# Two heads per weight block in the attention scores, and later contexts written inside the first steps

## The reference, cut to what matters

```python
x, xn = X, layernorm(X)                     # X: 32 batches x 256 tokens x 128
ctx = xn @ We.T                             # 16 columns
scores = einsum('bhqd,bhkd->bhqk', Q, K) * 8**-0.5 + 0.1 * ctx @ ctx.T   # 16 heads of 8 columns
attn = softmax(scores)
x = x + (attn @ V) @ Wo.T + top-2-of-8 expert layer(xn)                   # 128 -> 512 -> 128
```

## Time and profile before

| | |
|---|---|
| three executions | 710.49, 710.17, 706.68 us, median 710.17 |
| profiled execution | 709.09 us, its span 707.3 us |
| granted TensorE clock, mean | 0.979 |
| attention, batches 0 to 15 | about 80 to 303 us |
| experts | about 303 to 492 us |
| attention, batches 16 to 31 | about 492 us to the end |

### The profile page before, as it was taken

The page is one execution under the profiler, slowest core; times in us unless marked ns, Lnnn a source line. Parts: engine busy times, 40 slices in busy tenths (PEclk is TensorE's granted clock), DMA queues, the critical chain, the costliest instruction groups (busy, mean ns, idle before and its releaser), DMA issues.

```text
span 707.3 us, 24553 instructions
## 1 busy us (share of the span) xinstructions
PE 648.5 (92%) x7800; PEld 433.7 (61%) x7800; DVE 614.3 (87%) x1106; ACT 541.5 (77%) x1123; POOL 467.4 (66%) x542
## 2 busy tenths in 40 slices
PE   0377899999999999989999999999999999999996
PEld 0264345555555555579999999998455555555553
DVE  8989789899999999868888888888999999999991
ACT  2592378888888888788888888888778877878775
POOL 8680468676687757135565565565687888778774
PEclk9986799999999999999999999999999999999999
DMA  8859556766766766684554454452667788787742
GB/s 244 318 161 331 151 146 167 203 180 171 194 171 183 202 172 175 155 132 93 107 107 94 106 101 106 100 107 70 148 165 186 179 185 183 175 185 186 178 112 79
DMA packets 162948, 113.32 MB, mean 160 GB/s; under 512 B 72625, under 2 KB 150449, under 8 KB 162865
## 3 DMA queue, kind: packets, MB, share of 16 engines
q1 hardware_dynamic: 153632, 90.63, 52.5%
q0 software_dynamic: 8192, 16.86, 9.7%
q10 hardware_dynamic: 1040, 4.76, 1.8%
HBM read 55.42 MB, written 47.19 MB: 145 GB/s over the span
## 4 chain that ended last, share of the span: by engine, by line
PE 70%; DVE 12%; SPq 6%; DMA 4%; issue 4%; ACT 3%; ACTq 0%; DVEq 0%
PE bank L1133 14%; PE bank L1251 14%; PE bank L1111 13%; PE mx L1240 13%; PE mx L1145 8%; DVE mx L955 5%; DMA stack<-qk_dram 3%; PE bank L1031 3%; PE bank L1193 2%; DVE A L790 2%; PE bank L1155 1%; PE bank L1162 1%; ACT A L707 1%; SPq L318 1%; DMA stack<-mT 1%
## 5 line engine op out<-in xcount | busy, mean ns | idle before, releaser
L707 ACT ACTIVATE A<-bank 128x512 f32<-128x512 f32 x502 | 278.3, 597 | 63.6 <-PE bank L1133 55.9
L955 DVE TENSOR_REDUCE mx<-mx 128x4 f16<-128x1024 f32 x256 | 302.6, 1205 | 20.0 <-PE mx L1145 14.5
L578 POOL TENSOR_SCALAR rows<-rows,slot_p 128x128 f32<-128x128 f32 x142 | 112.0, 798 | 95.8 <-DVE rows L1008 95.8
L1133 PE MATMUL bank<-stack 113*128 113x256 f16 x1004 | 170.7, 277 | 1.7 <-ACT A L707 0.8
L564 POOL DMA_INDIRECT slots_x<-rows,pos x128 | 123.6, 966 | 52.9 <-PE bank L1133 34.0
L608 POOL DMA_INDIRECT rows<-slots_y,pos x128 | 121.3, 948 | 40.8 <-PE bank L1133 19.7
L1111 PE MATMUL bank<-A,V 128*32 128x256 f32 x2048 | 137.3, 386 | 1.7 <-ACT A L707 1.6
L751 ACT ACTIVATE rows<-mx,b 128x256 f32<-128x256 f32 x284 | 111.5, 474 | 25.7 <-PE mx L1240 23.9
L1133 PEld LDWEIGHTS bank<-stack 113*128 113x128 f16 x1004 | 72.9, 98 | 89.4 <-ACT A L707 56.4
L1000 DVE TENSOR_TENSOR rows<-rows 128x512 f16<-128x512 f32 x142 | 101.1, 713 | 25.1 <-ACT rows L755 22.6
L1251 PE MATMUL bank<-w,rows 128*128 x1704 | 107.3, 219 | 1.3 <-DVE rows L1000 1.3
(11 more groups left out here) (142 smaller groups left out, 596.2 us busy)
## 6 DMA issues: line engine op xcount, KB each, us to landing
stack<-ctx_rest SPq DMA_DIRECT2D x64, 256.0 KB
stack<-qk_dram SPq DMA_DIRECT2D x128, 96.0 KB
slots_y<-rows SPq DMA_DIRECT2D x71, 128.0 KB, 2.0
qk_dram<-hi_qk SPq DMA_DIRECT2D x64, 128.0 KB
stack<-ctx_high SPq DMA_DIRECT2D x128, 64.0 KB
slots_x<-A ACTq DMA_DIRECT2D x1, 4644.0 KB, 19.8
w_stage<-in_w SPq DMA_DIRECT2D x8, 512.0 KB
qk_dram<-lo_qk SPq DMA_DIRECT2D x64, 64.0 KB
```

What stands on the lines that cost most here:

```text
L578: ins = pool.tensor_scalar(ye[n % 4][:, h, :], ye[n % 4][:, h, :], slot_p[:, n // 4 % 3, n % 4, h:h + 1], None, ALU.mult)
L707: act.activation(A[:, n % NA, :, :].rearrange("p h s -> p (h s)"), scores(k, n)[:, :], ACT.Exp, scale=SCALE).then_inc(s_xp, 1)
L955: dve.tensor_reduce(mx[:, a, 8 * qt:8 * qt + 8].rearrange("q (i e w) -> q i e w", i=2, e=2)[:, :, g % 2], MX[u % 2][:, :].rearrange("q (i ...
L1133: mm = pe.matmul(scores(k, n)[:, i * S:(i + 1) * S], stack[0:SHIFT + 1, par, h, 1, c * P:(c + 1) * P], stack[0:SHIFT + 1, par, h, 0, :], s ...
```

## The change

`stack` becomes, per side, six blocks of four heads: four query blocks (one for each half and class) and two key blocks, one for each half. A key block holds, for w = 0 to 3, the keys of head w (class 0) on its rows and of head w+4 (class 1) on its rows. One matmul takes 128 keys of both as weights and streams 512 columns, head w's queries and then head w+4's; the zeros of each query side drop the other head's keys. A score tile has 512 columns as before; tile p of a pair now holds heads w and w+4 where it held two neighbours of one class, and the values pick them accordingly. The plain products keep their four matmuls.

`load` makes six transfers: `ctx_rest` to the queries (128 KB in runs of 512 bytes) and to the keys (64 KB in runs of 512 bytes) instead of one of 256 KB in runs of 1024 bytes; high contexts and projections as before in bytes, in runs of 2048 bytes. `context` writes `ctx_high` four times over instead of twice (1024 KB in all, before 768 KB). `part_c` has a buffer of its own. `context(1)`, `(2)` and `(3)` are issued at the end of the steps k = -1, 0 and 1, and SyncE waits for all of them at the end of step 1. All clears are issued by ScalarE, in two transfers, at the start. The first scatter of rows by GpSimd waits for 18 score tiles instead of 10.

```diff
-START = 4
+START = 8
-        qk_dram = nc.dram_tensor("qk_dram", [2, 3 * DK, H * 2 * S], ...)
-        ctx_high = nc.dram_tensor("ctx_high", [2, B // 2, 2 * DE, 2 * S], ...)
+        qk_dram = nc.dram_tensor("qk_dram", [2, 2, 3 * DK, H * S], ...)
+        ctx_high = nc.dram_tensor("ctx_high", [2, B // 2, 2 * DE, 4 * S], ...)
-        stack = sb("stack", [P, 2, H, 2, S], F16)
+        stack = sb("stack", [P, 2, 6, 4, S], F16)
+        part_c = sb("part_c", [P, 4, 2, 2 * S], F16)
...
+        def both_sides(row, n, par, g, i):
+            first_, second_ = 2 * g + i, 4 + g
+            return stack[row:row + n, par, first_:second_ + 1:second_ - first_, :, :]
...
-                    sp.dma_start(high, hi.to_broadcast([P, 2, S])).then_inc(s_cw[r], 16)
+                    sp.dma_start(high, hi.to_broadcast([P, 4, S])).then_inc(s_cw[r], 16)
...
             def load(half2, par2, g):
-                sp.dma_start(stack[REST:REST + 2 * DE, par2, 8 * g:8 * g + 8, :, :], rest).then_inc(s_st[par2][g], 16)
+                sp.dma_start(dst, rest[:, :, 0:S].to_broadcast([2 * DE, 8, S])).then_inc(s_st[par2][g], 16)
+                sp.dma_start(stack[REST:REST + 2 * DE, par2, 4 + g, :, :], rest[:, :, S:2 * S].to_broadcast([2 * DE, 4, S])).then_inc(s_st[par2][g], 16)
...
             write(0, 1, 1)
-            clear(sp, 8, 10)
             context(0)
             sp.wait_ge(s_cw[0], 96)
             for g in range(2):
                 load(0, 0, g)
             write(1, 2, 2)
-            clear(sp, 10, 14)
-            context(1)
-            clear(sp, 14, 16)
-            context(2)
-            context(3)
...
-                if k == 1:
-                    for r in range(1, 4):
-                        sp.wait_ge(s_cw[r], 96)
                 for g in range(2):
...
                         write(par3, n_hq, n_lq)
+                if k in (-1, 0, 1):
+                    context(k + 2)
+                if k == 1:
+                    for r in range(1, 4):
+                        sp.wait_ge(s_cw[r], 96)
...
-                pool.memset(stack[64:P, par, :, 1, :], -1.0).then_inc(s_post, 1)
+                pool.memset(stack[64:P, par, 4:6, :, :], -1.0).then_inc(s_post, 1)
...
             clear(act, 0, 8)
             for g in range(3):
                 normalise(g)
+            clear(act, 8, 16)
             root(1)
...
-                classes = stack[:, par].rearrange("r (a i h) s t -> r i a h s t", a=2, i=2)
+                classes = stack[:, par, 0:4].rearrange("r (a i) h t -> r i a (h t)", i=2)
                 dve.memset(classes[0:64, 1], 0.0)
-                ins = dve.memset(classes[64:P, 0, :, :, 0], 0.0)
+                ins = dve.memset(classes[64:P, 0], 0.0)
...
-                        for i in range(2):
-                            h = 8 * (g // 2) + 4 * p + 2 * (g % 2) + i
-                            mm = pe.matmul(scores(k, n)[:, i * S:(i + 1) * S], stack[0:SHIFT + 1, par, h, 1, c * P:(c + 1) * P], stack[0:SHIFT + 1, par, h, 0, :], start=True, stop=True)
-                        mm.then_inc(s_ex, 1)
+                        h, w = 8 * (g // 2), 2 * (g % 2) + p
+                        pe.matmul(scores(k, n)[:, :], k_side(par, h + w)[0:SHIFT + 1, c * P:(c + 1) * P], stack[0:SHIFT + 1, par, h // 4:h // 4 + 2, w, :], start=True, stop=True).then_inc(s_ex, 1)
```

More of the change, by code:

```diff
@@ L240, in scores, with q_side, k_side @@
             return ring[n % len(ring)] if k == B - 1 else EX[n % 2]
+        def q_side(par, h):
+            return stack[:, par, h // 4, h % 4, :]
+        def k_side(par, h):
+            return stack[:, par, 4 + h // 8, h % 4, :]
+        def both_sides(row, n, par, g, i):
+            first_, second_ = 2 * g + i, 4 + g
+            return stack[row:row + n, par, first_:second_ + 1:second_ - first_, :, :]
         def head_values(par, c, g, i):
@@ L314, in context @@
                 for q in range(2):
-                    lo, hi = (part_c[r][:, a:a + 1, q * S:(q + 1) * S] for a in range(2))
+                    lo, hi = (part_c[:, r, a:a + 1, q * S:(q + 1) * S] for a in range(2))
                     high, rest = (c[q, 4 * r:4 * r + 4].rearrange("i c (m t) -> (i c) m t", t=S) for c in (ctx_high, ctx_rest))
-                    sp.dma_start(high, hi.to_broadcast([P, 2, S])).then_inc(s_cw[r], 16)
+                    sp.dma_start(high, hi.to_broadcast([P, 4, S])).then_inc(s_cw[r], 16)
                     sp.dma_start(rest[:, 1:3], hi.to_broadcast([P, 2, S])).then_inc(s_cw[r], 16)
@@ L403, in attend @@
                     if g == 0 and f["p"]:
-                        n_hq, n_lq, n_st = (v if isinstance(v, int) else sp.to_reg(v) for v in (b3_ + 1, b3_ + 1, 80 * half3))
+                        n_hq, n_lq, n_st = (v if isinstance(v, int) else sp.to_reg(v) for v in (b3_ + 1, b3_ + 1, 96 * half3))
                         if k is None or b3_ >= 2:
@@ L700, in attend @@
                             if k == 0 and n == 0:
-                                act.wait_ge(s_zero, 64)
+                                act.wait_ge(s_zero, 32)
                             if k != 0 or g >= 2:
                                 act.wait_ge(s_pv, 4 * b + g - 1)
-                            if k == 0 and n == NA // 2:
-                                for sm in s_cw:
-                                    act.wait_ge(sm, 96)
                             act.activation(A[:, n % NA, :, :].rearrange("p h s -> p (h s)"), scores(k, n)[:, :], ACT.Exp, scale=SCALE).then_inc(s_xp, 1)
@@ L1110, in values @@
                         for i in range(4):
-                            mm = pe.matmul(PV[32 * i:32 * i + 32, 0:S], head_values(pp, c, g, i), A[:, (4 * g + 2 * c + i // 2) % NA, i % 2, :],
+                            mm = pe.matmul(PV[32 * i:32 * i + 32, 0:S], head_values(pp, c, g, i), A[:, (4 * g + 2 * c + i % 2) % NA, i // 2, :],
                                            start=(e == 0 and c == 0), stop=(e == 1 and c == 1))
@@ L1144, in plain @@
                                 h = 8 * (v // 4) + 4 * i + 2 * (v // 2 % 2) + p
-                                mm = pe.matmul(MX[v % 2][:, (2 * i + p) * S:(2 * i + p + 1) * S], stack[r0:r1, par1, h, 0, v % 2 * P:(v % 2 + 1) * P], stack[r0:r1, par1, h, 1, :],
+                                mm = pe.matmul(MX[v % 2][:, (2 * i + p) * S:(2 * i + p + 1) * S], q_side(par1, h)[r0:r1, v % 2 * P:(v % 2 + 1) * P], k_side(par1, h)[r0:r1, :],
                                                start=True, stop=True)
```

35 lines of the change are left out of this document (17 added, 18 removed).

## The result

The changed kernel takes 719.18 us (median of 4 executions, 718.45 to 721.4), the kernel before, run on the same chip, 710.33 us: ratio 1.0138, 95% interval 1.0116 to 1.016. The forecast was 708.9 us, with a range from 703.5 to 715. The profiled execution took 718.94 us, its span is 717.2 us, so it is 9.9 us above the span before.

The account below looks back on a forecast made before the run. VectorE was taken to bound about 28 of 32 steps, SyncE's queue the start. From the profiled 709.09 us, -3.8 at the start and +2.5 for contexts gave 707.8, or 708.9 us for the median; range 703.5 to 715.

Parts of the forecast that it names:

- steady steps and product: Steady steps stay at 13.2 us, VectorE at 12.4; the 512-column product, its weight loads already hidden, gains 0.
- the rivals of TensorE's: Steady steps: VectorE's gap closes, 14 us gained (chance 0.05), or weight loads aren't hidden, the skill's rule, 28 us (0.03).
- The scatters' 0: GpSimd's scatters start 8 score tiles later and cost nothing, GpSimd having nearly 3 us free in a step.
- six transfers at 0: Loads: one more issue, 0.4 us, covered by VectorE's 0.6 us, costs 0; rival: 8.4 us lost (chance 0.12).
- What the contexts cost in their new place: Contexts 2 and 3 make loads 1.7 and 2.0 us late; 2.5 us lost after cover, bounds 0 and 7.7.
- The contexts block the queue: Rival, SyncE's queue: issues at 0.96 us, two steps 7.7 us late in all, 714.7 us (chance 0.12).
- over 5 us of SyncE for a context: Sign, SyncE's queue: the prediction is wrong if a context takes over 5 us of SyncE.
- the start, -3.8 us: Before the steady steps: memsets 1.7, VectorE's earlier start 1.1 and TensorE's clock 1.0 gain 3.8 us together.
- Memsets, 1.7: First microseconds: halved memsets of VectorE and GpSimd gain 0 to 3.0 us, taken as 1.7; X must have landed.
- The clear moved to ScalarE, 0: Start: the larger clear on ScalarE's queue costs 0, its bytes flowing before and while context 0 is written.
- ScalarE held up between 18 and 33 us: Sign, start: the prediction is wrong if the second clear holds up ScalarE between 18 and 33 us.
- TensorE's stand, 1.1, and its clock, 1.0: Start of batch 1: TensorE's 3.39 us stand goes, VectorE starts 1.1 us earlier; keeping the clock gains 1.0 us.

Follow-up runs that it names:

- e10: e6 with the 512-column product made as two matmuls of 256 columns again: 710.62 us, ratio 1.0029 to the kernel before.
- e1: Changed kernel with clears and contexts 1 to 3 back in their old places; new layout, six transfers and 512-column product kept: 711.8 us, ratio 1.001.
- e8: e4 with the 128 KB transfer of each load cut in two, a seventh transfer: 721.82 us, ratio 1.0163.
- e4: Changed kernel with contexts 1 to 3 issued behind the first load of step -1, their wait at the start of step 1: 709.93 us, ratio 0.9989.
- e12: e4 with contexts 2 and 3 written once more, to unread memory without a wait, at the ends of steps 0 and 1: 715.5 us, ratio 1.0084.
- e11: e4 with the second clear cut in two, batch 3's slots cleared by ScalarE in step -1 at 69.9 us: 708.24 us, ratio 0.9982.
- e6: Changed kernel with contexts 1 to 3 before the steps, as in the kernel before; clears stay as changed: 710.3 us, ratio 1.0002.
- e5: e4 with ScalarE's second clear issued later, at 49 us: 711.55 us, ratio 1.003.
- e2: Changed kernel with ScalarE's second clear issued later, behind batch 1's projections: 714.92 us, ratio 1.0066.
- e3: Changed kernel with the wait for the contexts' landing put before the later loads instead of the end of step 1: 719.11 us, ratio 1.0105.
- e7: e4, but context 3 and the wait for it stay at the end of step 1: 716.89 us, ratio 1.0085.
- e13: e11 with context 3 issued by ScalarE at 65.0 us instead of by SyncE: 707.89 us, ratio 0.999.

## Why the prediction was wrong

**Right: steady steps and product.** The step is unchanged (13.20 us, VectorE 12.41); e10 shows the product's 0 in isolation, and with it that the rivals of TensorE's had nothing in them. The scatters' 0 was never tested alone; e1 contains it. On the rule of the Trainium skill that was weighed, "TensorE: Matmul & The Clock Gate", section "The mechanism", e10 bears too: the same weights loaded again for the second 256 columns, on the same rows, cost nothing in a steady step, so here the measurement goes against it. Where VectorE sets the pace this alone couldn't show the load hidden, but two score tiles take 0.61 us with four loads and 0.60 with two.

**Right, but narrowly: six transfers at 0.** e1 gives 0.1% with an interval from -0.1 to 0.3, and the steady steps in the second half have no loss. But e8 shows how little was left: the cover was thin, as the text said, and the next 0.4 us cost 4.4 us by the profiles, 11.9 by the medians.

**Wrong: "What the contexts cost in their new place", 2.5 us.** It is 6.9 us in the profiles (e4 against after), 9.3 by the medians. The failed step is how the two contexts were added up; the landing was too short as well. SyncE's queue, with e4 as the same kernel without the contexts there:

| us | e4 | e12, copies | after |
|---|---|---|---|
| load behind context 2 | 102.84 | 104.59 | 104.97 |
| load of the second half | 108.98 | 111.06 | 111.49 |
| `shift_rows` of that half over | 113.02 | 116.43 | 117.16 |
| load behind context 3 | 116.71 | 121.52 | 123.69 |
| first plain product of batch 4 | 123.0 | 126.6 | 129.4 |

Context 2 made the load 2.1 us late; I had said 1.7, and of it 1.0 us is lost up to batch 3 (14.4 us from batch 2 to 3, in e4 13.4), where I had 1.1. But I let that lateness end there, and gave context 3 the full pause of 3.3 us. In fact the lateness stays on the queue: 2.1, 2.5, and with one issue of 1.99 us 4.1 us late at 117.16, so that the pause (3.7 us in e4) is used up before context 3 begins. The issues of a context took 4.0 us, as I had 3.8. The landing was 2.5 to 2.9 us where I had 1.5 from context 0. So the load is late by 4.1 + 4.0 + 2.5 - 3.7 = 6.9 us, and 123.69 - 116.71 gives 7.0; of the second 0.6 us of cover nothing is seen. From e12, the queue without the landing is 5.7 of the 6.9 us, the landing with its wait 1.2. TensorE's clock was at half from 126.8 to 133.6 us, beginning in the stand of 4.70 us; what that cost is in the 6.9. The bound of 7.7 us for this term held in the profiles. The rival built on it ("The contexts block the queue") was right that the contexts block it, but put the cause in issues of 0.96 us each, and these took 0.67 (4.0 us for six). I had named over 5 us of SyncE for a context as a sign of being wrong: context 3 took 4.0, and 6.5 with its landing. What is not told apart is how much of the 5.7 us is SyncE's time and how much the 2 MB of bytes: the slow issues (1.99 us after, 2.16 in e12) and the load that follows a step later (3.74 us to land in e12) look like the bytes.

**Wrong: the start, -3.8 us.** Batch 2 begins 0.8 us later than before. By its terms:
- *Memsets, 1.7.* They ended early, but the condition I had named came in: X lands at 8.56 us. The statistics' first operation on 16 columns ends at 12.37 instead of 13.12, so 0.75.
- *The clear moved to ScalarE, 0.* "Its bytes flow before and while context 0 is written" was the failed sentence: they flow also while batch 0's projections are written, transfers in small pieces that everything behind them waits for. The last of them lands at 47.27 us; in the kernel before its last piece starts at 39.4. It makes batch 0's products 3.8 us late (e4 against e11). My sign for it, ScalarE held up between 18 and 33 us, looked in the wrong stretch: it stood from 43.6 to 47.35.
- *TensorE's stand, 1.1, and its clock, 1.0.* The stand did go. But the stretch from 72 to 82 us now runs at half clock; the clock gave nothing. That the late batch 0 is the reason isn't shown: e6's is as late (64.2 us), and there TensorE had 0.50 only from 71.0 to 74.4 us and 1.00 behind. Nor does an early batch 0 pay in full: e11 wins 3.8 us there and keeps 2.2, e5 wins 4.7 and loses 1.7.

The rest: the new layout's three steps are 41.9 us in e4 and 42.1 in e1 against 40.4 before, but 40.7 in e6. In e4 the load from 116.71 ends with a landing of 3.85 us. I didn't find what makes this differ between kernels with the same loads; since e1's and e4's profiles are the slowest of their ten executions, it may be no more than that. The sum closes on the profile: start 0.8 + contexts 6.9 + this 1.5 + later steps 0.9 - 0.2 behind the last = 9.9 us.

## What to carry to other kernels

A queue that issues in order keeps its lateness: add up each moved issue along the queue to the next real pause, and count a pause once, for all that was put ahead of it. A large transfer that "nobody waits for" is not free where the engines are full: look in the windows for its stretch's DMA share, and for small transfers on the critical path beside it. And look for a pause before moving work: twelve issues cost 7 us or more inside the steps and nothing that could be measured behind the first load of step -1, where SyncE had waited 13.9 us for VectorE.

## What the runs showed of the hardware

Two queues at work at once shared the engines by pieces, not by bytes: from 37 to 39 us of the changed kernel's trace 156 pieces of batch 0's high write (512 bytes, about 27 ns each) go beside 158 pieces of the clear (4,644 bytes, about 184 ns each). So the 256 KB of the two high writes took from 36.9 to 43.8 us beside a queue of large pieces; in the kernel before they took 1.1 us. Why their first piece started only 3.7 us after the issue (0.8 us before the change) the trace doesn't show: the clear alone was at work then. The Trainium skill ("DMA: Bandwidth & Descriptors", section "Queues, rings and completion order") says that each engine takes its queues in turn, packet by packet; by that rule a queue of small pieces falls behind one of large pieces, and from 37 to 39 us this trace agrees, with its pieces nearly one for one. The page's packet holds several descriptors; how many pieces an engine takes in one turn the counts can't tell. A SyncE issue, 0.3 to 0.7 us for the most part, took up to 6.62 us beside the same clear (e2). And in the kernels whose batch 4 came late behind the contexts (after, e2, e3, e7, e12) TensorE's clock was at half for 3.4 to 6.8 us between 122 and 134.4 us; in e4, e6, e11 and e13, where it didn't, the clock stayed at full speed there.
